# A 64-image vision tower on one core: weight loads on another queue, a later weight fold, loads one slot ahead, and separate orders for the last slots

## The reference, cut to what matters

```python
# x: 64 images, 3 x 196 x 196.  196 patches of 14 x 14 x 3 per image, 128 channels, 197 tokens
tokens = einsum('bsd,hd->bsh', patches, W) + b
h = concatenate([cls, tokens], axis=1) + pos
# linear attention with a decaying state, as one causal 197 x 197 weighting per image
h = h + (scan over the state of (x@Wk+bk), (x@Wv+bv), (x@Wq+bq), x = layernorm(h)) @ Wo + bo
# routed attention: per image one of three weight sets (8, 4 or 1 key heads of 16)
x = layernorm(h)
sel = argmax(softmax(relu(mean(x) @ r_w1 + r_b1) @ r_w2 + r_b2))
h = h + softmax(q k^T / 4) v @ wo[sel]        # 8 heads, 197 x 197 scores each
```

## Time and profile before

| what | value |
|---|---|
| median of 3 executions | 843.01 us (841.98 to 844.24) |
| the profiled execution: its own time | 847.23 us |
| the profiled execution: its span | 845.5 us |
| PE busy | 786.9 us, 93% of the span |
| DVE, ACT, POOL busy | 580.2, 602.9, 401.0 us |
| mean granted clock of PE | 0.972 of full speed |

### The profile page before, as it was taken

One profiled execution on the slowest core, in us unless ns is written; L12 is line 12 of the kernel. 1 busy time (PEld: TensorE's weight loads), 2 busy tenths in 40 slices (PEclk: granted clock), 3 DMA queues, 4 the chain that ended last, 5 costly groups with the idle time before them and its releaser, 6 DMA issues.

```text
span 845.5 us, 25686 instructions
## 1 busy us (share of the span) xinstructions
PE 786.9 (93%) x8496; PEld 663.6 (78%) x8496; DVE 580.2 (69%) x1842; ACT 602.9 (71%) x1364; POOL 401.0 (47%) x954
## 2 busy tenths in 40 slices
PE   3777899999999999999999999999999999889886
PEld 2566688888888888888888888888888888767664
DVE  3245677777777777777787777777777877755541
ACT  3456478887788777887877887778878786645553
POOL 1357565555545464555555455655555455411000
PEclk9989899999999999999999999999999999997997
DMA  5545645455555555555555545555555553222200
GB/s 141 142 124 170 181 150 170 139 160 165 162 164 150 150 165 170 160 160 143 160 167 164 165 144 157 161 169 165 150 151 164 167 162 110 89 89 82 90 14 15
DMA packets 138704, 120.53 MB, mean 143 GB/s; under 512 B 12606, under 2 KB 138446, under 8 KB 138574
## 3 DMA queue, kind: packets, MB, share of 16 engines
q1 hardware_dynamic: 136898, 118.34, 47.5%
q10 hardware_dynamic: 1676, 0.57, 0.3%
HBM read 30.99 MB, written 6.46 MB: 44 GB/s over the span
## 4 chain that ended last, share of the span: by engine, by line
PE 83%; DVE 5%; SPq 3%; issue 2%; POOL 2%; ACT 1%; DMA 1%; ACTq 1%; POOLq 1%; DVEq 0%
PE ps L432 12%; PE ps L623 11%; PE ps L572 9%; PE ps L600 7%; PE ps L605 5%; PE ps L545 4%; PE ps L652 4%; PE ps L559 4%; PE ps L503 3%; PE ps L634 3%; PE ps L496 3%; DVE top L841 2%; PE ps L546 2%; PE ps L475 2%; PE ps L515 2%
## 5 line engine op out<-in xcount | busy, mean ns | idle before, releaser
L841 DVE TENSOR_REDUCE top<-ps 99x2 f32<-99x394 f32 x512 | 265.2, 560 | 118.8 <-PE ps L572 118.3
L977 ACT ACTIVATE prob<-ps 99x396 f32<-99x396 f32 x512 | 233.1, 497 | 71.4 <-PE ps L605 71.1
L915 ACT ACTIVATE packed<-img 84x686 f32<-84x686 f32 x128 | 177.9, 1398 | 0.1
L432 PE MATMUL ps<-cols,w_tok 126*128 126x196 f32 x640 | 126.5, 344 | 8.8 <-DMA cols<-packed 7.6
L600 PE MATMUL ps<-top_rows,pick_rows 64*99 64x198 f32 x1024 | 121.1, 267 | 3.0 <-ACT prob L977 3.0
L432 PEld LDWEIGHTS ps<-cols,w_tok 126*128 126x128 f32 x640 | 114.3, 199 | 10.0 <-DMA cols<-packed 8.6
L605 PE MATMUL ps<-stack 64*99 64x198 f32 x1024 | 115.2, 256 | 0.0
L572 PE MATMUL ps<-stack 64*99 64x198 f32 x1024 | 106.9, 288 | 5.2 <-DVE top L841 5.1
L600 PEld LDWEIGHTS ps<-top_rows,pick_rows 64*99 64x99 f32 x1024 | 86.7, 166 | 24.1 <-issue 19.8
L623 PE MATMUL ps<-prob,v_ones 99*32 99x198 f32 (+1 forms) x2048 | 100.9, 337 | 0.1
L366 POOL TENSOR_SCALAR xhat<-h,mv,rstd 99x128 f32<-99x128 f32 x114 | 90.1, 799 | 5.9
(11 more groups left out here) (148 smaller groups left out, 1563.2 us busy)
## 6 DMA issues: line engine op xcount, KB each, us to landing
stack<-qk SPq DMA_DIRECT2D x256, 198.0 KB, 2.4
img<-in_x SPq DMA_DIRECT2D x192, 150.1 KB
cols<-packed SPq DMA_DIRECT2D x128, 160.8 KB
cols<-packed SPq DMA_DIRECT2D x64, 128.6 KB
out<-h SPq DMA_DIRECT2D x64, 49.5 KB
out<-h SPq DMA_DIRECT2D x64, 49.0 KB
w_rows<-in_L_tok_W SPq DMA_DIRECT2D x1, 294.0 KB, 3.4
sets<-in_L_ffn_wo SPq DMA_DIRECT2D x3, 64.0 KB
```

Source lines behind the costliest of these rows:

```text
L432: last = nc.tensor.matmul(ps[:, CY, 0:N * N], w_tok[0:KROWS, s, :], cols[b.ring % 2][:, :, s, :], start=(s == 0), stop=(s == STEPS - 1))
L841: nc.vector.tensor_reduce(top[:, c // 4, first:first + 2], columns, AX.X, ALU.max, negate=True).then_inc(m_read, 1)
L915: last = nc.scalar.activation(packed[b.ring % 2][:, first:end, :], img[b.ring % IMGS][:, :].rearrange("p (x w) -> p w x", w=P)[:, first:en ...
L977: nc.scalar.activation(prob[:, c, :], ps[0:T, E0 + c % 2, 0:CHUNK], ACT.Exp, scale=DK ** -0.5).then_inc(exp_done, 1)
```

## The change

Five things are changed.

1. The seven transfers of the attention weights and biases (4 of 64 KB, 3 of 0.5 KB) move from the head of ACT's queue to the head of POOL's, ahead of POOL's first instruction. The four transfers of feed-forward set 0 move from SP's queue (slot 2) to POOL's, behind its constants.
2. PE's fold of the attention weights moves behind the first three of the five steps of image 0's `patches`; its scratch bank is E0 in place of CY. ACT packs image 1 before it waits for the fold.
3. SP issues image 0's load ahead of its wait for the pads, and in slot n loads image n+1 in place of n.
4. In the filling slots `attend_out` writes bank M0 in place of CZ, so that `turn_patches` waits for `u_ready` (long past) and not for DVE's addition (`h1_ready`).
5. From slot 69 (DRAINED = B + ADDED) PE, DVE and ACT follow lists of their own.

The core of the diff:

```diff
-HEAD = 3
+HEAD, LOADED, FFN = 3, 1, 2
+DRAINED = B + ADDED
...
             sp.dma_start(w_rows[:, :], ins["L0_tok_W"]).then_inc(w_rows_in, 16)
-            sp.wait_ge(img_padded, 2)
...
-                plan = [(gather, n.back(GATHERED)), (stack_up, n.back(STACKED)), (store, n.back(STORED)), (load, n)]
+                plan = [(gather, n.back(GATHERED)), (stack_up, n.back(STACKED)), (store, n.back(STORED)), (load, n.back(-LOADED))]
...
+            for i in range(LOADED):
+                load(Image(0, i))
+            sp.wait_ge(img_padded, 2)
...
         def _(pool):
+            for to, name in ((w_raw[0], "Wq"), (w_raw[1], "Wk"), (w_raw[2], "Wv"), (wo_attn, "Wo")):
+                pool.dma_start(to[:, :], ins[f"L0_attn_{name}"]).then_inc(attn_pool, 16)
+            for to, name in zip(b_raw, ("bq", "bk", "bv")):
+                pool.dma_start(to[:, :], column(ins[f"L0_attn_{name}"])).then_inc(attn_pool, 16)
...
             pool.wait_ge(half_ready, 1)
+            for to, name in ((raw[0][0][:, :], "wq0"), (raw[0][1][:, :], "wk0"), (set_of[:, 2, :], "wv0"), (set_of[:, 3, :], "wo0")):
+                pool.dma_start(to, ins[f"L0_ffn_{name}"]).then_inc(ffn_pool, 16)
...
             def turn_patches(b):
-                if added.exists():
+                if added.exists() and b.i + PATCHED < MAXED:
+                    pe.wait_ge(u_ready, added.i + 1)
+                elif added.exists():
                     pe.wait_ge(h1_ready, added.i + 1)
...
+                draining = [
+                    (mix_values, ending, 0), (key_scores, mixing, 0), (max_scores, maxed, 0), (mix_values, ending, 1),
+                    (key_scores, mixing, 1), (max_scores, maxed, 1), (row_mix, ending), (project_qk, projected),
+                    (route_hidden, routing), (key_scores, mixing, 2), (max_scores, maxed, 2), (turn_mixed, ending),
+                    (route_logits, routing), (turn_top, topped), (project_v, topped), (project_out, ending),
+                    (key_scores, mixing, 3), (max_scores, maxed, 3),
+                ]
-                for step, b, *which in filling if n.i < MAXED else plan:
+                for step, b, *which in filling if n.i < MAXED else draining if n.i >= DRAINED else plan:
                     if b.exists():
                         step(b, *which)
+                if n.i == PATCHED - 1:
+                    fold_weights()
...
+                if n.i >= DRAINED:
+                    plan = [(maximum, maxed, 0), (maximum, maxed, 1), (choose, choosing), (maximum, maxed, 2),
+                            (maximum, maxed, 3), (normalise, ending), (route_relu, routing), (low_halves, projected),
+                            (maximum, maxed, 4), (route_bias, routing), (maximum, maxed, 5), (finish, ending),
+                            (maximum, maxed, 6), (maximum, maxed, 7), (split_top, maxed)]
...
+            pack(Image(0, 1), 0)
+            pack(Image(0, 1), 1)
             act.wait_ge(pe_step, 4)
...
+                if n.i >= DRAINED:
+                    plan = [(exponent, mixing, 0), (exponent, mixing, 1), (keep_mix, ending), (exponent, mixing, 2),
+                            (exponent, mixing, 3), (high_halves, projected), (exponent, mixing, 4), (keep_mixed_t, ending),
+                            (route_exp, routing), (top_row, topped), (exponent, mixing, 5), (exponent, mixing, 6),
+                            (exponent, mixing, 7), (keep_v, topped)]
```

More of the change, by code:

```diff
@@ L297, in _ @@
             pool.wait_ge(half_ready, 1)
+            set_of = sets[:, 0:4 * D].rearrange("p (w e) -> p w e", w=4)
+            for to, name in ((raw[0][0][:, :], "wq0"), (raw[0][1][:, :], "wk0"), (set_of[:, 2, :], "wv0"), (set_of[:, 3, :], "wo0")):
+                pool.dma_start(to, ins[f"L0_ffn_{name}"]).then_inc(ffn_pool, 16)
             def build_set(i):
                 if i == 0:
-                    pool.wait_ge(ffn_in, 16 * 16)
+                    pool.wait_ge(ffn_pool, 16 * 4)
+                    pool.wait_ge(ffn_in, 16 * 12)
                 for n in KV[i:i + 1]:
@@ L411, in _, with fold_weights @@
             last.then_inc(pe_step, 1)
[L412 to L425, removed]
-            pe.wait_ge(w_tok_ready, 1)
+            pe.wait_ge(w_tok_ready, 1)
+            def fold_weights():
+                pe.wait_ge(attn_pool, 16 * 7)
+                for k in range(3):
+                    last = nc.tensor.transpose(ps[:, E0, k * D:(k + 1) * D], w_raw[k][:, :], ident[:, :])
+                last.then_inc(pe_step, 1)
+                pe.wait_ge(dve_step, 2)
+                for t in range(2):
+                    last = nc.tensor.matmul(ps[0:T, CZ, t * T:(t + 1) * T], power_wide[:, t, :], ident[0:T, 0:T],
+                                            start=True, stop=True)
+                last.then_inc(pe_step, 1)
+                pe.wait_ge(dve_step, 3)
+                nc.tensor.matmul(ps[:, CW, 0:D], w_bias[1][:, :], w_bias[0][:, :], start=True, stop=True)
+                nc.tensor.matmul(ps[:, CW, D:2 * D], w_bias[2][:, :], wo_attn[:, :], start=True, stop=True).then_inc(pe_step, 1)
+                pe.wait_ge(pads_ready, 1)
+                pe.wait_ge(picks_ready, 1)
             def patches(b, first=0, end=STEPS):
@@ L501, in attend_out @@
                 pe.wait_ge(u_ready, b.i + 1)
+                bank = M0 if b.i + ADDED < MAXED else CZ
                 for t in range(2):
-                    last = nc.tensor.matmul(ps[0:T, CZ, t * D:(t + 1) * D], ut[:, t * T:(t + 1) * T], w_vo[:, :],
+                    last = nc.tensor.matmul(ps[0:T, bank, t * D:(t + 1) * D], ut[:, t * T:(t + 1) * T], w_vo[:, :],
                                             start=True, stop=True)
@@ L584, in turn_top @@
                     pe.wait_ge(log_ready, batch_of(routed))
-                elif b.has(1):
+                else:
                     pe.wait_ge(top_ready, b.i)
@@ L721, in _ @@
             for k in range(3):
-                last = nc.vector.tensor_reduce(w_shift[:, k:k + 1], ps[:, CY, k * D:(k + 1) * D], AX.X, ALU.add)
+                last = nc.vector.tensor_reduce(w_shift[:, k:k + 1], ps[:, E0, k * D:(k + 1) * D], AX.X, ALU.add)
             last.then_inc(dve_inner, 1)
@@ L730, in _ @@
             for k in range(3):
-                last = nc.vector.tensor_scalar(w_bias[k][:, :], ps[:, CY, k * D:(k + 1) * D], w_shift[:, k:k + 1], None,
+                last = nc.vector.tensor_scalar(w_bias[k][:, :], ps[:, E0, k * D:(k + 1) * D], w_shift[:, k:k + 1], None,
                                                ALU.subtract)
@@ L773, in add_attention @@
                 dve.wait_ge(kept, b.i + 1)
-                nc.vector.tensor_tensor(h1[b.ring][:, :, :], two(ps[0:T, CZ, 0:2 * D]), h1[b.ring][:, :, :], ALU.add).then_inc(h1_ready, 1)
+                bank = M0 if b.i + ADDED < MAXED else CZ
+                nc.vector.tensor_tensor(h1[b.ring][:, :, :], two(ps[0:T, bank, 0:2 * D]), h1[b.ring][:, :, :], ALU.add).then_inc(h1_ready, 1)
                 dve.wait_ge(add_ready, 1)
@@ L897, in _ @@
         def _(act):
-            for to, name in ((w_raw[0], "Wq"), (w_raw[1], "Wk"), (w_raw[2], "Wv"), (wo_attn, "Wo")):
-                act.dma_start(to[:, :], ins[f"L0_attn_{name}"]).then_inc(attn_in, 16)
-            for to, name in zip(b_raw, ("bq", "bk", "bv")):
-                act.dma_start(to[:, :], column(ins[f"L0_attn_{name}"])).then_inc(attn_in, 16)
             for t in range(2):
@@ L1008, in slot @@
                 turned, added, patched = n.back(TURNED), n.back(ADDED), n.back(PATCHED)
-                arrived = n.back(PACKED) if n.i > PACKED else Image(-1, 0)
+                arrived = n.back(PACKED) if n.i > PACKED + 1 else Image(-1, 0)
                 projected, topped, mixing, ending = n.back(PROJECTED), n.back(TOPPED), n.back(MIXING), n.back(ENDING)
```

19 lines of the change are left out of this document (11 added, 8 removed).

## The result

| | before | changed |
|---|---|---|
| median | 843.62 us (841.98 to 847.20, 6 runs) | 822.62 us (820.56 to 823.41, 6 runs) |
| profiled execution: span | 845.5 us | 821.7 us |
| mean granted clock | 0.972 | 0.989 |

The ratio is 0.9743 (95%: 0.972 to 0.9767): 21.0 us faster, where 22 were forecast. The total came out within 2 us of the forecast, but by two errors that cancel: the drain gave 5 us more than I had put down, and the start 5 us less.

What follows compares the result with a forecast made beforehand. PE is busy throughout full slots, so only both ends can gain: 845.5 - 17.0 (drain) - 5.2 (start) = 823.3 us of span; with the gain taken from the median, 821 us, own range 815 to 827.

Steps and rivals of the forecast that it cites:

- The draining slots: Slots 69 to 78: the same work reordered fills PE's waits; 100.64 us becomes 83.6, a gain of 17.0 us.
- the walk through the order: One draining slot stepped through in its new order at 2.4 GHz: 7.7 us, taken as 7.9 for slots 71 to 73.
- small rests: Short leftover waits of PE in slots 71 to 73, for which 7.7 us was taken as 7.9.
- a bound: PE's busy time in slot 72, 7.79 of 9.50 us, taken as the least such a slot can take.
- Slot 70's new wait: PE reaches `project_qk` before the routing's weights are in `w_in`: 2.2 us lost, slot 70 takes 10.2 us.
- The clock: Drain: slots 71 to 73 at clock 1.00, but two stretches at 1.2 GHz, 1.4 us each, added to 80.8 us.
- The start: ACT's queue freed of seven issues, first gather at 9.4 or 10 us, gather 4 earlier: gain 5.2 us, bounds 0 and 7.
- Loads one slot ahead: Steady part: loads one slot ahead wait for a packing that is one slot older; effect nothing.
- POOL's issues: Head of POOL's queue: seven issues delay its identity, PE's first transposes and `w_tok`; price taken as 1.0 us each.
- the free range: Price per issue on POOL, up to 1.37 us, at which the seven issues delay nothing needed at 14.1 us.
- the rivals that lived from slow issues, 826 and slower: POOL's issues at 2 us or more: start gives about nothing, 826 us, chance 0.17; dearer still, slower overall, chance 0.05.

Runs made afterwards that it cites:

- e11: Changed kernel with DVE dividing the mixture ahead of maxima 2 and 3 in the draining slots: 827.42 us in one run.
- e7: Changed kernel with `project_qk` behind the turn of the mixture in slot 70 alone: 820.81 us, ratio 0.9699.
- e3: Changed kernel with ACT's rows (bias, position, token) issued only once the token weights have landed: ratio 0.9732.
- e5: Changed kernel without the lists for the slots from 69 on, so only the start changed: 845.98 us, ratio 1.0009.
- e8: Changed kernel with two loads ahead of the first gather, ACT's rows held and the fold ahead of image 0's patches: 817.02 us, ratio 0.9643.
- e9: Changed kernel with two loads first, ACT's rows held, fold ahead of image 0's patches, and slot 70's `project_qk` behind the mixture's turn: 815.49 us, ratio 0.9659.
- e1: Changed kernel with two images' loads ahead of the first gather and not three: ratio 0.9738.
- e4: Kernel before with only the lists for the slots from 69 on and the waits they need: 820.84 us, ratio 0.9694.
- e6: Changed kernel with the fold of the attention weights back ahead of image 0's patches: 822.31 us, ratio 0.9711.

## Why the prediction was right in sum, and where it was wrong

**The draining slots: right in mechanism, undersized.** The term was 17.0 us and measured 21.9. By slot, forecast and measured: 69, 8.9 and 8.22; 70, 10.2 and 11.00 (with the low-clock stretch in it; 9.6 by the 1.4 us that I had priced one at); 71 to 73, 7.9 and 7.44; 74 and 75, 7.4 and 7.24; 76, 6.7 and 6.69; 77, 7.0 and 6.87; 78, 9.5 and 9.14. The slots sum to 80.8 forecast and 78.7 measured, and the 78.7 hold the one low stretch that came; I had added two, 2.8 us, on top. In the walk through the order, the "small rests" between 7.7 and 7.9 don't exist, and the walk's own 7.7 already lay under the 7.79 that I had called a bound. In slots 71 to 73 the wait for `mixed` is 0 and that for the maxima 0, as forecast; e11 shows that the one for the maxima (0.54 us) returns when DVE's order is turned back. Still, PE's busy time per slot (7.36) fell below that 7.79. I took the busy time of a slot with waits for PE's work; it was not, since it shrank with the waits. The work is the same: each of these slots has 100 matmuls, and the counts of 104 and 102 take in those that reach over a cut.

**Slot 70's new wait: right, a little oversized.** Forecast 2.2 us, measured 1.82; from the start of `choose` to the end of the weight copy 2.97 us (753.93 to 756.90), forecast 3.0. e7 shows that it can be avoided.

**The clock: right for slots 71 to 73, wrong in count.** I had put in two low stretches and one came. Slots 71 to 77 stayed at 1.00. In slot 70, behind PE's wait of 1.82 us, the clock fell: from 758.50 to 762.20 it is 0.54, nearly all at 1.2 GHz, and `project_v` takes 1.06 us where it takes 0.60 in slot 71. In e7, without that wait, the same slot shows 1.00. Slot 78 was at 0.72, which its forecast (from the earlier trace rows, 0.68) holds already. What decides is not shown: in the kernel before, slots 71 and 72 have the same order and the same two waits, and one was at 0.84, the other at 1.00. The Trainium skill ("TensorE: Matmul & The Clock Gate", "A second HAM failure mode") tells of a kernel whose clock swings between its levels because PE is idle for short times between groups of matmuls. This trace agrees: the mean clock of the drain went from 0.86 to 0.95 when the waits were closed.

**The start: the step that failed is the first.** I wrote that "ACT is 3.38 us earlier and the first gather goes out at 9.4 instead of 12.75, or at 10 if image 0 lands late". It went out at 15.81. I treated seven issues taken from ACT's queue as time won and did not ask what then leaves that queue earlier: its rows, 296 KB in seven transfers, which now share the DMA engines with the token weights and image 0. e3 shows the image there by 8.83 when they are held. Everything behind followed the forecast, shifted: columns 1.95 us after the last issue (1.8), fold 4.0 (3.84), gather 4 at 46.02 (39.8, that is 6.2 later, as the columns, 20.32 for 14.1). Gain of the start 5.2 forecast; e5 measured none (ratio 1.0009).

**Loads one slot ahead.** I priced them as harmless. With early images they are not: e3 against e8 and e9, 6.1 us against at most 2.3 and 1.93 for the same gather. In the changed kernel itself the gather went out at 15.81, its columns came 1.95 us after the last issue, and the third load cost nothing (e1: the same time). That it had landed by then is my reading; the trace does not give its landing.

**POOL's issues: inside the free range.** 0.55 us and not 1.0, so the identity is ready before DVE's token weights, and the rivals that lived from slow issues, 826 and slower, have no ground. The Trainium skill ("DMA: Bandwidth & Descriptors", "Anatomy of one DMA") gives about 2.0 us fixed per transfer. In my estimate from that page of the Trainium skill I let POOL be held for all of it, 14 us for seven, and it was held for 4.0 (1.36 to 5.38). The Trainium skill itself puts most of the 2.0 us there down to the completion, not to the issue, so this was a misreading of mine.

**What stays open.** In e4 slot 15 is reached at 124.06, 3.0 us before the kernel before, which has the same code there. In the changed kernel image 4 is reached 2.0 us later than before (50.41 for 48.43), and slot 15 all the same 0.24 us earlier. The filling slots from image 4 on differ in mean clock between executions (0.92 before, 0.96 changed, 0.98 in e4), and so single traces say nothing of 2 us at the start. The third load was not left out alone while the rows are held, which would give its price without the fold's. Set 0 on POOL's queue and the filling slots' change of wait and bank were not taken back one by one; e5 has them only together with the rest.

## What to carry to other kernels

When issues leave a queue, ask what the queue sends earlier in their place and what that shares: at the start of this kernel the DMA engines were full, and freeing a queue brought the wrong transfers forward. Take an engine's busy time in a slot with waits as an upper figure for its work, not as the least that a slot can take: PE's shrank by about 5% when the waits closed (7.79 to 7.37, 7.17 to 6.83). Waits that stand in a row (image, columns, fold) are tested together, since each alone showed nothing here.

## What the runs showed that I had not expected

- DMA engines at a busy share of 1.0 for 10 us moved 163 to 183 GB/s in the changed kernel. In the same stretch of e6 (share 1.0), seven transfers that POOL had issued by 5.4 us, 64 KB at most, were there only at 13.26.
- ACT's rows (seven transfers of at most 49.5 KB), issued from 0.82 us on, delayed image 0, which SP issued from 1.29 us on: packed at 12.46 to 13.35 us with them early, at 8.83 to 10.70 when they wait for the token weights.
- An issue on POOL took 0.55 us for 64 KB as for 0.5 KB, about what an issue takes on ACT.
- PE's busy time for the same matmuls in slot 72 fell from 7.79 to 7.37 us at the same clock of 1.00, once nothing waited between them.
